# Inverse deviations and softmax numerators as elementwise powers on GpSimd instead of ScalarE functions

## What is computed

```python
def _ln_c(v, eps=1e-06):                       # over the 64 channels; _ln_t: the same per token, eps=1e-05
    return (v - mean(v)) / jnp.sqrt(var(v) + eps)
x = x + conv3x3(fake_quant(_ln_c(x)), fake_quant(w))       # blocks of 16 values, powers of two as scales
t = _to_tokens(x)
xf = _ln_t(t)
probs = softmax(xf @ gate_w + gate_b)          # 8 experts
cw = top-2 of probs, the rest zero
t = t + sum over e of cw[e] * (gelu(xf @ W1[e] + b1[e]) @ W2[e] + b2[e])
```

## Time and profile before

| | us |
|---|---|
| median of 3 runs | 212.49 |
| lowest, highest | 212.31, 212.99 |
| the profiled execution | 214.55 |
| its span in the trace | 212.7 |
| busy in the span: PE, DVE, ACT, POOL | 168.8, 143.7, 116.9, 124.6 |

### The profile page before, as it was taken

The page is one execution under the profiler, slowest core; times in us unless marked ns, Lnnn a source line. Parts: engine busy times, 40 slices in busy tenths (PEclk is TensorE's granted clock), DMA queues, the critical chain, the costliest instruction groups (busy, mean ns, idle before and its releaser), DMA issues.

```text
span 212.7 us, 4043 instructions
## 1 busy us (share of the span) xinstructions
PE 168.8 (79%) x1211; PEld 85.0 (40%) x1211; DVE 143.7 (68%) x456; ACT 116.9 (55%) x153; POOL 124.6 (59%) x118
## 2 busy tenths in 40 slices
PE   2977202990089965979989999999999999999880
PEld 2974201360046753435434444344444444444330
DVE  0899999404998879965957748758487486254262
ACT  2359700233213783844796676676766676777730
POOL 7697006630196613423677677777777777677483
PEclk9999655797559996799999999999999999999998
DMA  5940000000000000494992975949929738649701
GB/s 181 312 80 3 0 2 0 0 3 0 0 0 0 3 0 0 107 212 95 199 192 70 230 164 149 207 99 221 224 85 206 171 121 178 150 115 200 182 0 49
DMA packets 16178, 22.39 MB, mean 105 GB/s; under 512 B 2202, under 2 KB 7970, under 8 KB 16162
## 3 DMA queue, kind: packets, MB, share of 16 engines
q1 hardware_dynamic: 16002, 22.04, 44.8%
q10 hardware_dynamic: 160, 0.15, 0.3%
HBM read 19.82 MB, written 2.36 MB: 104 GB/s over the span
## 4 chain that ended last, share of the span: by engine, by line
PE 53%; DVE 19%; DMA 9%; issue 8%; ACT 5%; POOL 2%; SPq 1%; POOLq 1%; DVEq 1%; ACTq 0%
PE ps L1056 21%; PE ps L1073 20%; PE ps L985 8%; DMA gbc<-gate_rows 5%; DVE ssum L618 3%; DVE xn L630 3%; DMA gate_rows<-gateT 2%; DMA cw<-in_conv_w 2%; POOL qpad L355 1%; SPq L276 1%; PE ps L1012 1%; ACT hl L493 1%; DVE topi L807 1%; PE ps L942 1%; DVE gbc L693 1%
## 5 line engine op out<-in xcount | busy, mean ns | idle before, releaser
L403 POOL TENSOR_TENSOR x<-x,y_sb 128x512 f32 (+1 forms) x63 | 80.1, 1271 | 40.1 <-DVE y_sb L846 36.8
L546 ACT ACTIVATE work<-ps,bias_sb,w_back 128x1024 f32<-128x1024 f32 x64 | 76.9, 1203 | 37.2 <-PE ps L1056 36.9
L846 DVE SCALAR_TENSOR_TENSOR y_sb<-ps,bias_sb,gbc 128x512 f32<-128x512 f32 x64 | 47.6, 748 | 41.3 <-PE ps L1073 33.3
L1073 PE MATMUL ps<-work,w_sb 128*64 128x512 f32 x256 | 65.6, 593 | 1.2 <-DVE y_sb L846 1.1
L1056 PE MATMUL ps<-xT,w_hi 128*64 128x512 f16 x256 | 39.5, 389 | 0.6 <-ACT work L546 0.6
L1056 PE MATMUL ps<-xT,w_lo 128*64 128x512 f16 x256 | 39.0, 385 | 0.0
L985 PE MATMUL ps<-qpad,cw_bd 128*128 128x512 bf16 x72 | 21.2, 453 | 21.5 <-POOL qpad L355 21.5
L1056 PEld LDWEIGHTS ps<-xT,w_hi 128*64 128x64 f16 x256 | 13.5, 111 | 33.0 <-issue 30.7
L1073 PEld LDWEIGHTS ps<-work,w_sb 128*64 128x64 f32 x256 | 17.9, 137 | 14.1 <-issue 2.6
L985 PEld LDWEIGHTS ps<-qpad,cw_bd 128*128 128x128 bf16 x72 | 7.7, 109 | 32.5 <-issue 15.6
L1056 PEld LDWEIGHTS ps<-xT,w_lo 128*64 128x64 f16 x256 | 14.8, 112 | 13.7 <-issue 1.0
(11 more groups left out here) (106 smaller groups left out, 179.2 us busy)
## 6 DMA issues: line engine op xcount, KB each, us to landing
gbc<-gate_rows SPq DMA_DIRECT2D x16, 768.0 KB, 10.0
gbc<-gate_rows SPq DMA_DIRECT2D x16, 256.0 KB, 4.0
x_sb<-in_x SPq DMA_DIRECT2D x8, 256.0 KB, 4.9
out<-x SPq DMA_DIRECT2D x8, 256.0 KB, 9.8
w_raw<-in_W SPq DMA_DIRECT2D x2, 256.0 KB, 5.9
w_sb<-in_W SPq DMA_DIRECT2D x1, 256.0 KB
gate_rows<-gateT SPq DMA_DIRECT2D x8, 32.0 KB, 2.0
cw<-in_conv_w ACTq DMA_DIRECT2D x2, 72.0 KB, 3.9
```

What stands on the lines that cost most here:

```text
L403: pool.tensor_tensor(x2[:, ds(c * W, W)], x2[:, ds(c * W, W)], y_sb[:, u % H_RING, :], ALU.add).then_inc(added, 1)
L546: act.activation(h_sb[:, u % H_RING, :], bank(H + 2 * (u % 2), 2 * W), ACT.Gelu, bias=b1_sb[:, u:u + 1], scale=w_back[:, u:u + 1]).then_in ...
L846: dve.scalar_tensor_tensor(y_sb[:, u % H_RING, :], bank(Y + u % 2), b2_sb[:, u:u + 1], gbc[:, slot, u, :], ALU.add, ALU.mult).then_inc(wei ...
L1073: last = pe.matmul(ps[r * CH:(r + 1) * CH, (Y + u % 2) * W:(Y + u % 2 + 1) * W], w2_sb[:, u, :], h_sb[:, u % H_RING, r * W:(r + 1) * W], s ...
```

## The change

Six steps move between engines. The two roots and two inversions of layer norm 1, and the three and three of layer norm 2, become on GpSimd a `tensor_scalar` (variance plus eps) and, after a `link`, a `tensor_tensor` with the operation `pow` and an exponent tile of -0.5 (`inverse_deviations`). The three exponentials become one `tensor_tensor` `pow` each, with a tile filled with e as base (`exponentials`). Both tiles are filled at the start. ScalarE keeps squares, copies and gelus, VectorE loses its five reciprocals. Two loops of GpSimd are written out so that the new steps can stand between their turns; the semaphores `std1` and `std2` go.

```diff
             pool.memset(eps1[:, :], LN1_EPS)
+            pool.memset(inv_half[:, :], -0.5)
+            pool.memset(euler[:, :], EULER)
             pool.memset(eps2[:, :], LN2_EPS).then_inc(eps_ready, 1)
...
+            def inverse_deviations(part, summed, eps, inverted):
+                first, last = part
+                n = (last - first) * GROUPS
+                pool.wait_ge(summed, last)
+                link(pool.tensor_scalar(std[:, first:last, :], ssum[:, first:last, :], 1.0 / CH, eps, ALU.mult, ALU.add))
+                pool.tensor_tensor(rstd[:, first:last, :].rearrange("p c g -> p (c g)"),
+                                   std[:, first:last, :].rearrange("p c g -> p (c g)"), inv_half[:, 0:n],
+                                   ALU.pow).then_inc(inverted, 1)
+
+            def exponentials(k):
+                first, last = LOGIT_PARTS[k]
+                n = (last - first) * GROUPS * EXPERTS
+                pool.wait_ge(z_ready, k + 1)
+                e = ex[:, first:last, :, :].rearrange("p z g e -> p (z g e)")
+                pool.tensor_tensor(e, euler[:, 0:n], e, ALU.pow).then_inc(exp_ready, 1)
...
             for k in range(3, len(E2M1_MIDS)):
                 last = pool.tensor_scalar(cw_steps[:, k, :], cw_a[:, :], E2M1_MIDS[k], 1.0, ALU.is_ge, ALU.mult)
+                if k == 4:
+                    inverse_deviations(LN1_PARTS[0], ss1, LN1_EPS, rstd1)
             link(last)
+            inverse_deviations(LN1_PARTS[1], ss1, LN1_EPS, rstd1)
...
-            with pool.Fori(4, NCH - 1) as c:
+            for c in range(4, NCH - 1):
                 quantised(c)
                 residual(c - 2)
+                if c == 5:
+                    inverse_deviations(LN2_PARTS[0], ss2, LN2_EPS, rstd2)
             quantised(NCH - 1)
+            inverse_deviations(LN2_PARTS[1], ss2, LN2_EPS, rstd2)
...
-            with pool.Fori(0, EARLY) as c:
-                wait_alone(pool, (xh_ready, c + 1))
+            for c in range(2):
+                pool.wait_ge(xh_ready, c + 1)
                 low_half(c)
-            with pool.Fori(EARLY, NCH) as c:
-                wait_alone(pool, (xh_by_dve, c + 1 - EARLY))
+            inverse_deviations(LN2_PARTS[2], ss2, LN2_EPS, rstd2)
+            for c in range(2, EARLY):
+                pool.wait_ge(xh_ready, c + 1)
                 low_half(c)
+                if c == 2:
+                    exponentials(0)
+            for c in range(EARLY, NCH):
+                pool.wait_ge(xh_by_dve, c + 1 - EARLY)
+                low_half(c)
+                if c == NCH - 3:
+                    exponentials(1)
...
             for u in range(UNITS):
                 add_unit(0, u)
+                if u == 3:
+                    exponentials(2)
```

More of the change, by code:

```diff
@@ L42 @@
 AMAX_FLOOR = 1e-30
+EULER = 2.718281828459045
 WSCALE = 2.0 ** 13
@@ L108, in program @@
         eps2 = sb("eps2", [128, 1])
+        inv_half = sb("inv_half", [128, NCH * GROUPS])
+        euler = sb("euler", [128, NCH * GROUPS * EXPERTS])
         NW = EXPERTS * HIDDEN
@@ L174, in program @@
         ss1 = sem("ss1")
-        std1 = sem("std1")
         rstd1 = sem("rstd1")
@@ L194, in program @@
         ss2 = sem("ss2")
-        std2 = sem("std2")
         rstd2 = sem("rstd2")
@@ L422, in square @@
                 act.activation(work[:, ds(c * W, W)], bank(c), ACT.Square).then_inc(squared, 1)
-            def deviations(part, summed, eps, ready):
-                first, last = part
-                act.wait_ge(summed, last)
-                act.activation(std[:, first:last, :], ssum[:, first:last, :], ACT.Sqrt,
-                               bias=eps[:, 0:1], scale=1.0 / CH).then_inc(ready, 1)
             act.wait_ge(eps_ready, 1)
-            act.activation(std[:, 0, 0:1], eps1[:, 0:1], ACT.Sqrt)
             for c in range(NCH):
                 square(c, cent1, sq1)
-                if c == 4:
-                    deviations(LN1_PARTS[0], ss1, eps1, std1)
-            deviations(LN1_PARTS[1], ss1, eps1, std1)
             def take_v(c):
@@ L501, in take_xT @@
                                ACT.Copy).then_inc(xT_by_act, 1)
-            def exponentials(k):
-                first, last = LOGIT_PARTS[k]
-                act.wait_ge(z_ready, k + 1)
-                act.activation(ex[:, first:last, :, :], ex[:, first:last, :, :], ACT.Exp).then_inc(exp_ready, 1)
             def take_gateT(c):
@@ L531, in _ @@
             square(7, cent2, sq2)
-            deviations(LN2_PARTS[2], ss2, eps2, std2)
-            exponentials(0)
             take_xT(2)
@@ L536, in _ @@
             take_gateT(0)
-            exponentials(1)
             def gelus(c, gates_after=2):
@@ L553, in _ @@
             gelus(0, gates_after=3)
-            exponentials(2)
-            act.activation(std[:, 0, 0:1], eps1[:, 0:1], ACT.Gelu)
             with act.Fori(1, NCH - 1) as c:
@@ L619, in reduce_squares @@
                                   by_group(work[:, ds(c * W, W)]), AX.X, ALU.add).then_inc(summed, 1)
-            def invert(parts, k, deviations, inverted):
-                first, last = parts[k]
-                dve.wait_ge(deviations, k + 1)
-                dve.reciprocal(rstd[:, first:last, :], std[:, first:last, :]).then_inc(inverted, 1)
             def normalise(c, parts, inverted, ready):
@@ L888, in _ @@
             route_copy(0)
-            invert(LN2_PARTS, 2, std2, rstd2)
             route_max(range(GROUPS))
```

7 lines of the change are left out of this document (removed).

## The result

| | us |
|---|---|
| before, median of 4 runs | 212.74 (212.31 to 214.18) |
| after, median of 4 runs | 310.50 (309.67 to 311.91) |
| ratio, 95% interval | 1.456 (1.449 to 1.464) |
| the profiled execution of after, its span | 310.32, 308.5 |

The change costs 97.8 us; between the two spans (212.7 and 308.5) it is 95.8, since the profiled execution of before lay 2 us over its median. The prediction counted from 212.49, the median of three of the four runs of before. Some executions are slow, over 1.5% above the fastest of their kernel: the ratios with an interval leave them out, the medians in this document do not. First the page of after: the busy times of the engines, and the shares of the chain that ended last.

What follows compares the result with a forecast made beforehand. GpSimd was taken to set the pace early, a chain through several engines from 76 us. 0.6 + 6.0 + 12.4 + 7.8 + 13.9 = 40.7 us gave 253 us; range 217 to 304, likeliest case 232 to 277.

Steps and rivals of the forecast that it cites:

- What bounds the kernel: GpSimd sets the pace before the expert stage, its early delays arriving in full; from 76 us a chain through several engines decides.
- The price of a power: GpSimd's time for each element of a power: 60 ns taken, bounded between 2.1 and 144 ns.
- the sum: All parts' delays added, 40.7 us at 60 ns an element; each ns of price moves it by 0.61 us.
- a dear power: Rival: a power's dependent steps cost 121 to 144 ns an element, giving 290 to 304 us; chance 0.30.
- Layer norm 1: GpSimd's inverse deviations before the weights' sums: 6.0 us later, passing both idle pairs in full; 0.6 more for tile fills.
- Layer norm 2, first two parts, nothing: Powers around the last two quantised chunks on GpSimd: no cost, since 3.2 us of cover hides the first pair.
- Third part and first exponential: Low halves 2 and 3 wait on GpSimd for the last sum, then the exponential delays chunk 0's gates: 12.4 us.
- Second exponential: GpSimd's power for chunks 2 and 3 holds VectorE from route_copy, delaying the gates of chunk 1: 7.8 us.
- Third exponential: GpSimd's 256-element power delays an addition, routing and the sixth weighing, less 1.5 us of table loads returned: 13.9 us.
- The rule of the Trainium skill: VectorE instructions with two SBUF inputs block against GpSimd's reading SBUF; without it some 14 us of the sum would go.
- the power's code has to be fetched: Rival: GpSimd must first fetch the power's code, 6.3 us there and back for eight powers: over 304 us; chance 0.02.
- Cheaper or faster: Rivals: power of 5 to 25 ns, 219 to 232 us, 0.13; under 5 ns, 217 to 219, 0.03; faster, 210, 0.02.

Runs made afterwards that it cites:

- plain_op: Kernel after with a multiplication in place of every power, order and waits unchanged: 222.23 us.
- half_pow: Kernel after with each power on only the first half of its elements, the other deviations multiplied, the other shifted logits left as they are: 260.99 us.
- the ladder: Kernel after with exponentials given back to ScalarE: the third 275.34 us, second and third 259.11, all three 241.90.
- probe: Kernel before with powers, a multiplication and a long addition on GpSimd added at its end, VectorE operations beside the first power and the addition: 371.76 us.
- one_stop: Kernel before with GpSimd's maximum over partitions put right behind its broadcast, and VectorE's weight maxima ahead of the convolution's weights: 204.71 us, 0.961 of before.

## Why the prediction was wrong

The time lies 6.5 us above the range's upper end of 304. By the prediction's own steps:

**What bounds the kernel** was right. GpSimd's delay before 20 us came through both pairs of idle time in full (13.4 at L360, 14.1 at chunk 4), and from 76 us the chain through low halves, logits and routing decided.

**The price of a power** is the step that failed, and the term that was mis-sized: 60 ns an element taken, 160 measured. By the prediction's own slope of 0.608 us a ns the 100 ns are 60.8 us, and the forecast of 253 was 57.5 too low. Also the upper end, 144, was under it. The count of 30 to 40 steps and the rows of the operations over partitions were both no evidence for it; no row of before bounded it from above. The rest of the sum can be judged apart from the price, because three prices were run:

| ns an element | the sum's loss | measured, between spans |
|---|---|---|
| 2.1 (`plain_op`, a multiplication) | 5.5 | 6.9 |
| 80 (`half_pow`) | 52.9 | 47.2 |
| 160 (after) | 101.5 | 95.8 |

The profiled execution of before lay some 2 us over its median; between medians the loss is 9.5, 48.3 and 97.8 us. The sum is 40.7 + 0.608 x (price - 60). Its slope held between 80 and 160; its level is some 6 us too high there (4 to 5 between medians). With the right price it says 314 us where 310.5 was measured. The rival "a dear power", at 0.30, was right that the price is high, though its range too ended at 144; its reason, steps that depend on one another, no run shows.

**Layer norm 1**: 0.6 and 6.0 predicted; two powers of 5.45 us and not 2.10 make it 0.6 + 6.0 + 6.7 = 13.3, and it was 13.4. Right but for the price.

**Layer norm 2, first two parts, nothing**: with powers of 2.96 and 2.92 us the cover named there was not enough. The last wait for sums ended at 94.16 (L339), the sums of before at 77.52: 16.6 against 14.1 at chunk 4, so 2.5 us came through. It grows with the price: the same two rows come 3.5 and 3.1 us later in `plain_op` (61.33 and 80.65), so nothing came through, and 10.4 and 11.8 later in `half_pow` (68.23 and 89.33), so 1.4 did.

**Third part and first exponential**: the order was right. With the power of 5.42 us the shifted logits should come 5.1 + 3.3 = 8.4 later from here, and it was 25.6 - 16.6 = 9.0. From them to the gates it should be 7.3 + 12.9 = 20.2, and was 45.2 - 25.6 = 19.6.

**Second exponential**: the place was wrong. The prediction had VectorE held from route_copy on, so that the routing of chunk 1 waited. It was not held: route_copy (L797 at 131.28) took 0.18 us beside the power, and the gates of chunk 1 were no later than those of chunk 0. What waited was GpSimd's own queue, low halves 6 and 7, and TensorE for them: 14.91 us in the profile, 16.2 in the ladder. At 160 ns the prediction's reading would have cost 7.8 + 12.8 = 20.6.

**Third exponential**: also here VectorE ran on, which the prediction named as what would prove it wrong. It had said that without the hold only the ring of four would stop the weighing, and some 14 us of the sum would go: all that it had for this part. By its own numbers that was too much: of a power of 15.5 us the ring covers less than 7. The ring holds four units of 1.72 us, less than 7, and the power took 41.24. So 35 us, because the ring was full and not because VectorE was held; the table loads given back are in it and were not measured apart. At 160 ns the prediction's way gives 13.9 + 25.6 = 39.5, 4.3 too much. With the 4.4 too much of the second exponential, less the 2.5 that layer norm 2 was not given and the small misses of the other two parts, this is the 5.7 us by which the sum is too high at the right price.

**The rule of the Trainium skill** (page "SBUF — State Buffer", section "Who interferes with whom"), by which a VectorE instruction with two SBUF inputs contends with a GpSimd one that reads SBUF, for ports that only one of them can hold, was weighed there in favour of the sum. `probe` agrees for an addition (6.88 us) and disagrees for a power (1.13 us): the measurement decides. From L829 in the earlier trace rows, which stood beside an addition, the prediction had concluded for all of GpSimd's instructions. The other page cited ("GPSIMD Engine Reference", section "Performance pitfalls for Q7 kernels") gave an estimated 100 ns for 30 dependent steps; by its figure 160 ns would be an estimated 48 of them. The estimate by that page, 277, was nearer than the forecast of 253, and still 33 us short; no run shows how many steps a power has.

**The remaining rivals**: that the power's code has to be fetched did not happen (the gap before L340 is that of the link, 0.08 us). Cheaper or faster: `plain_op` shows that even a multiplication in those places costs 3 to 4%.

## What to carry to other kernels

An operation for which no row of the trace has a price is measured first, by a kernel that does it at its end: here one row of 20.8 us would have ended the question, and the price taken from a count of steps was short by a factor of 2.7. On GpSimd an elementwise power belongs only on a few elements a partition, off the path: 32 inverse roots a partition cost 5.4 us, while a multiplication of 128 elements costs 0.45. A step put into an engine's queue also costs what it waits for, whatever its own price: look at which short instructions stand behind it and who idles for them.

## What the runs showed of the hardware

- GpSimd's `tensor_tensor` with `pow` takes 160 ns for each element of a partition and 0.3 us to start, on 16, 64 or 128 partitions and with a base of 1.5 or of one.
- GpSimd's instructions differ in what they do to VectorE. Beside an addition of 7.01 us an operation of VectorE with two SBUF inputs took 6.88 us; beside a power 1.13 us, where the same shape takes 0.68 with one input from PSUM, and with both in SBUF while GpSimd idles (L722). What the 0.45 us more are was not tried.
- The idle time on GpSimd before and behind an operation over partitions (5.91 and 6.71 us, 6.27 and 7.01 in the kernel before) comes once for two such operations that follow each other (`one_stop`: 5.54, then 0.29 and 0.52 us of work, then 7.18).
- Behind an idle stretch of 33 us, with a granted clock of 0.54, TensorE had a mean of 0.60 for its first 4.3 us of work and 1.00 from 213 us on; this restart cost 1.7 us.
